# A fused linear-attention and routed-FFN block: output products in fp32r terms with streamed weights, and a third head's mask on ScalarE

## The reference

```python
# attention: 16 heads of 16, feature width 64
q, k, v = heads(x @ Wq + bq), heads(x @ Wk + bk), heads(x @ Wv + bv)
qp, kp = relu(q @ rw) + EPS, relu(k @ rw) + EPS          # per head
kv = kp.T @ v                                            # summed over the whole sequence
out = (qp @ kv) / (qp @ kp.sum() + EPS)
x = layernorm(x + out @ Wo + bo)
# FFN: gated MLP of width 1024, plus experts
sim = (x @ Wq) . keys                # 2 halves x 4 heads x 64 keys
sx, sy = top_8 of each half;  scores = top_8 of the 64 sums sx + sy      # per head
w = silu(x @ down_embed[idx]) * softmax(scores)          # 4 heads x 8 experts of 1024
y = (silu(x @ Wg + bg) * (x @ Wu + bu)) @ Wd + bd  +  sum of w * up_embed[idx]
x = layernorm(x + y)
```

## Time and profile before

| | us |
|---|---|
| median of 3 runs | 3515.26 (3514.70 to 3517.06) |
| the profiled execution | 3515.04, its span 3513.3 |
| PE busy | 3414.6 (97%) |
| DVE busy | 2830.2 (81%) |
| ACT busy | 1990.0 (57%) |
| POOL busy | 1163.0 (33%) |
| output products, lines 744 and 746 | 622.3 and 609.1 of PE's busy time |
| chain that ended last | PE 81%, DVE 8%, ACT 6%, POOL 2% |

### The profile page before, as it was taken

One profiled execution on the slowest core, in us unless ns is written; L12 is line 12 of the kernel. 1 busy time (PEld: TensorE's weight loads), 2 busy tenths in 40 slices (PEclk: granted clock), 3 DMA queues, 4 the chain that ended last, 5 costly groups with the idle time before them and its releaser, 6 DMA issues.

```text
span 3513.3 us, 49408 instructions
## 1 busy us (share of the span) xinstructions
PE 3414.6 (97%) x18400; PEld 2693.9 (77%) x18400; DVE 2830.2 (81%) x5316; ACT 1990.0 (57%) x2886; POOL 1163.0 (33%) x724
## 2 busy tenths in 40 slices
PE   8779999999999999999999999999999999999988
PEld 6457877777877777877777877777777778777777
DVE  4688888888888888888888887888878888888873
ACT  4456556555566555556555655555655564555551
POOL 0233333333333333333333333333333333343330
PEclk9899999999999999999999999999999999999999
DMA  4000000000000000000000000000000000000000
GB/s 121 18 13 19 7 13 19 19 19 19 7 13 19 19 19 14 12 13 19 19 19 9 17 13 19 19 19 7 19 13 19 19 13 7 13 13 7 12 7 12
DMA packets 23452, 60.84 MB, mean 17 GB/s; under 512 B 5808, under 2 KB 10160, under 8 KB 23216
## 3 DMA queue, kind: packets, MB, share of 16 engines
q1 hardware_dynamic: 23216, 57.69, 5.0%
HBM read 40.91 MB, written 16.78 MB: 16 GB/s over the span
## 4 chain that ended last, share of the span: by engine, by line
PE 81%; DVE 8%; ACT 6%; issue 3%; POOL 2%; DMA 0%; SPq 0%; POOLq 0%; DVEq 0%; ACTq 0%
PE ring L651 25%; PE y_bank L744 11%; PE y_bank L746 10%; PE step_bank L553 6%; PE step_bank L545 5%; PE step_bank L651 4%; PE step_bank L589 3%; PE step_bank L581 3%; PE step_bank L680 3%; DVE prob L1144 3%; PE step_bank L670 3%; PE step_bank L724 3%; PE step_bank L539 2%; POOL grid L464 2%; PE y_bank L740 1%
## 5 line engine op out<-in xcount | busy, mean ns | idle before, releaser
L464 POOL TENSOR_TENSOR grid<-ex 128x1024 f32<-128x1024 f32 x512 | 997.6, 1956 | 1507.5 <-ACT ex L877 730.6
L744 PE MATMUL y_bank<-wd_sb,gate 128*128 128x256 f32 x2048 | 622.3, 386 | 1.7 <-DVE wexp L1166 1.7
L746 PE MATMUL y_bank<-up_sb,wexp 128*128 128x256 f32 x2048 | 609.1, 379 | 0.0
L1144 DVE SCALAR_TENSOR_TENSOR prob<-grid,narrow,prob 128x1024 f32<-128x1024 f32 x256 | 552.2, 2157 | 9.0
L651 PE MATMUL ring<-x1T_hl,downT_hl 128*128 128x512 f32 x1536 | 420.8, 409 | 16.8 <-ACT gate L901 16.7
L651 PE MATMUL ring<-x1T_hl,wg_hl 128*128 128x512 f32 x1536 | 431.2, 416 | 3.8 <-DVE gate L1160 3.8
L1131 DVE SCALAR_TENSOR_TENSOR grid<-grid,best 128x1024 f32<-128x1024 f32 x256 | 327.2, 1278 | 131.8 <-POOL grid L464 128.8
L746 PEld LDWEIGHTS y_bank<-up_sb,wexp 128*128 128x128 f32 x2048 | 389.2, 190 | 53.0
L651 PE MATMUL ring<-x1T_hl,wu_hl 128*128 128x512 f32 x1536 | 421.4, 409 | 0.0
L744 PEld LDWEIGHTS y_bank<-wd_sb,gate 128*128 128x128 f32 x2048 | 354.0, 190 | 53.3 <-issue 25.2
L651 PEld LDWEIGHTS ring<-x1T_hl,wu_hl 128*128 128x128 f32 x1536 | 282.0, 188 | 119.8 <-issue 42.9
(11 more groups left out here) (169 smaller groups left out, 5578.7 us busy)
## 6 DMA issues: line engine op xcount, KB each, us to landing
xb<-in_L_attn_x SPq DMA_DIRECT2D x34, 512.0 KB, 3.5
out_y<-x SPq DMA_DIRECT2D x32, 512.0 KB, 2.9
xa<-in_L_attn_x SPq DMA_DIRECT2D x30, 512.0 KB, 4.2
prob<-in_L_ffn_down_embed SPq DMA_DIRECT2D x1, 1024.0 KB, 6.0
prob<-in_L_ffn_Wg SPq DMA_DIRECT2D x1, 1024.0 KB, 8.8
prob<-in_L_ffn_Wu SPq DMA_DIRECT2D x1, 1024.0 KB, 10.9
wd_sb<-in_L_ffn_Wd SPq DMA_DIRECT2D x1, 1024.0 KB, 11.3
up_sb<-in_L_ffn_up_embed SPq DMA_DIRECT2D x1, 1024.0 KB, 11.8
```

Source lines behind the costliest of these rows:

```text
L464: pool.tensor_tensor(grid[:, h % 2], bcast(ex[:, h, 0:NX].unsqueeze(2), [P, NX, NK]), bcast(ex[:, RH + h, 0:NK].unsqueeze(1), [P, NX, NK]) ...
L744: pe.matmul(rows, gate[:, c % 2, t * P:(t + 1) * P], wd_sb[:, c, :], start=(c == 0 and t % 2 == 0), stop=False, skip_group_check=True)
L746: mm = pe.matmul(rows, wexp[:, c % 2, t * P:(t + 1) * P], up_sb[:, c, :], start=False, stop=(c == C - 1), skip_group_check=True)
L1144: ins = dve.scalar_tensor_tensor(out=row, in0=g, scalar=rz[:, h:h + 1], in1=row, op0=ALU.mult, op1=ALU.add, accum_out=mass[:, 0:1] if h == ...
```

## The change

Both output products are made of three fp32r terms. Per chunk there are 12 gate terms (four tiles: high x high, high x low, low x high) and behind them 12 terms of the expert weight, instead of four tiles with one fp32 product of each kind. The splits of `gate` and `wexp` are made in each slot: `gate_top(c)` and `wexp_top(c-1)` are casts by ACT, `ff_low` is DVE's difference. The gate's low part stands behind `ff_wexp(c)` on DVE; the expert weight's stands at the head of the next slot, ahead of `ff_h`, but for chunk 7, where it is made in slot 7 itself, with its cast ahead of the mask of head 1. `gate` and `wexp` themselves lie in free parts of `prob`, and the masks get waits for them.

Wd and up_embed split take twice the room. They are split in the prologue (eight rounds of cast, low part and store, PREP_STEPS = 18), kept in a DRAM tensor, and streamed back, one chunk of 512 KB at a time into a ring of two slots, by transfers that POOL issues (`ff_stream`), each at the head of a slot and behind the wait that chunk c-2 has been used.

ACT masks head 2 too, right behind head 1. DVE's keep of head 2 goes; its add becomes a plain add and moves from behind add 1 to behind keep 3.

```diff
@@ -46,7 +46,7 @@
-    ACT_HEADS, STEEP = 2, float(2 ** 30)
+    ACT_HEADS, STEEP = 3, float(2 ** 30)
@@ -87,7 +87,8 @@
-        wd_sb, up_sb = sb("wd_sb", P, C, D), sb("up_sb", P, C, D)
+        wdup = sb("wdup", P, 2, 4, D, dt=F32R)
+        wdup_kept = nc.dram_tensor("wdup_kept", [C, P, 4, D], F32).ap()
@@ -119,20 +120,31 @@
-        gate = sb("gate", P, 2, G)
-        wexp = sb("wexp", P, 2, G)
+        gate_hi, gate_lo = sb("gate_hi", P, 2, G, dt=F32R), sb("gate_lo", P, 2, G, dt=F32R)
+        wexp_hi, wexp_lo = sb("wexp_hi", P, 2, G, dt=F32R), sb("wexp_lo", P, 2, G, dt=F32R)
...
@@ -345,9 +364,11 @@
-        PREP_STEPS, PREP_WG, PREP_WU = 11, 9, 10
+        PREP_STEPS, PREP_WG, PREP_WU = 18, 9, 10
+        PREP_WD = {11: (0,), 12: (1,), 13: (2,), 14: (3,)}
+        PREP_UP = {14: (0,), 15: (1,), 16: (2,), 17: (3,)}
...
-        W_ALL = 16 * (4 + 4 + 2 + 4 + 2)
+        W_ALL = 16 * (4 + 2 + 2 + 4 + 2)
@@ -380,6 +401,14 @@
+            sp.wait_ge(prep_full, 4)
+            sp.dma_start(wd_rows, Wd.rearrange("(c p) n -> p c n", p=P)).then_inc(wd_staged, 16)
+            sp.wait_ge(low_ready, 2)
+            sp.dma_start(up_rows, up.rearrange("(c p) n -> p c n", p=P)).then_inc(up_staged, 16)
+            for w, i in [(0, 0), (0, 1), (0, 2), (0, 3), (1, 0), (1, 1), (1, 2), (1, 3)]:
+                sp.wait_ge((wd_low, up_low)[w], i + 1)
+                sp.dma_start(wdup_kept[2 * i:2 * i + 2, :, 2 * w:2 * w + 2, :].rearrange("c p w d -> p c w d"),
+                             wdup[:, :, 2 * w:2 * w + 2, :].bitcast(F32)).then_inc((wd_kept, up_kept)[w], 16)
@@ -470,9 +499,20 @@
+                def ff_stream(c):
+                    g = n * C + c
+                    if g == 0:
+                        pool.wait_ge(wd_kept, 16 * (C // 2))
+                        pool.wait_ge(up_kept, 16 * (C // 2))
+                    wait(pool, y_full, g - 1)
+                    pool.dma_start(wdup[:, c % 2], wdup_kept[c]).then_inc(wdup_loaded[c % 2], 16)
...
+                    if ff:
+                        ff_stream(c)
@@ -725,15 +765,19 @@
-                def ff_out(c, pair):
-                    if pair == 0:
+                def ff_out(c, half):
+                    first, last = c == half == 0, c == C - 1 and half == 1
+                    if half == 0:
...
-                        pe.wait_ge(h_ready, n * C + c + 1)
-                        pe.wait_ge(*drained("pt", n, c))
-                    for t in (2 * pair, 2 * pair + 1):
-                        rows = y_bank[pair][:, (t % 2) * D:(t % 2 + 1) * D]
-                        if c == C - 2:
+                        pe.wait_ge(wdup_loaded[c % 2], 16 * ((n * C + c) // 2 + 1))
+                        pe.wait_ge(gate_split, n * C + c + 1)
+                    else:
+                        pe.wait_ge(wexp_split, n * C + c + 1)
+                    hi, lo = ((gate_hi, gate_lo), (wexp_hi, wexp_lo))[half]
+                    for t in range(T):
+                        rows = y_bank[t // 2][:, (t % 2) * D:(t % 2 + 1) * D]
+                        if c == C - 2 and half == 0:
@@ -741,11 +785,11 @@
-                        pe.matmul(rows, gate[:, c % 2, t * P:(t + 1) * P], wd_sb[:, c, :],
-                                  start=(c == 0 and t % 2 == 0), stop=False, skip_group_check=True)
-                        mm = pe.matmul(rows, wexp[:, c % 2, t * P:(t + 1) * P], up_sb[:, c, :],
-                                       start=False, stop=(c == C - 1), skip_group_check=True)
-                    if pair == 1:
+                        for i, (src, w) in enumerate([(hi, 0), (hi, 1), (lo, 0)]):
+                            mm = pe.matmul(rows, src[:, c % 2, t * P:(t + 1) * P], wdup[:, c % 2, 2 * half + w, :],
+                                           start=(first and t % 2 == 0 and i == 0), stop=(last and i == 2),
+                                           skip_group_check=True)
+                    if half == 1:
@@ -799,6 +843,16 @@
+                for i in PREP_WD.get(k, ()):
+                    act.wait_ge(wd_staged, 16)
+                    wait(act, wd_kept, 16 * i)
+                    act.copy(wdup[:, :, 0, :], wd_rows[:, 2 * i:2 * i + 2, :]).then_inc(wd_high, 1)
+                for i in PREP_UP.get(k, ()):
+                    act.wait_ge(up_staged, 16)
+                    wait(act, up_kept, 16 * i)
+                    act.copy(wdup[:, :, 2, :], up_rows[:, 2 * i:2 * i + 2, :]).then_inc(up_high, 1)
+                if k > PREP_WU:
+                    return
@@ -887,10 +941,13 @@
-                    g = grid[:, h].rearrange("p a b -> p (a b)")
+                    g = grid[:, h % 2].rearrange("p a b -> p (a b)")
...
+                        act.wait_ge(wexp_split, (s - 1) * C)
+                    if t == 2 and h == 0 and ff:
+                        act.wait_ge(wexp_split, n * C + C // 2)
@@ -898,12 +955,22 @@
-                    act.activation(gate[:, c % 2], ring[c % 2][:], ACT.Silu,
+                    if c == 0:
+                        wait(act, wexp_split, n * C)
+                    act.activation(gate(par, c), ring[c % 2][:], ACT.Silu,
...
-                    act.activation(wexp[:, c % 2], ring[c % 2][:], ACT.Silu).then_inc(ring_act, 1)
+                    act.activation(wexp(par, c), ring[c % 2][:], ACT.Silu).then_inc(ring_act, 1)
+                def gate_top(c):
+                    act.wait_ge(h_ready, n * C + c + 1)
+                    act.copy(gate_hi[:, c % 2], gate(par, c)).then_inc(gate_high, 1)
+                def wexp_top(c):
+                    act.wait_ge(*drained("pt", n, c))
+                    act.copy(wexp_hi[:, c % 2], wexp(par, c)).then_inc(wexp_high, 1)
@@ -911,6 +978,8 @@
                         ff_gate(c)
+                        if c:
+                            wexp_top(c - 1)
                     if at:
@@ -921,11 +990,14 @@
                         ff_dots(c)
+                        gate_top(c)
                     if at:
...
                             at_use(*use)
+                    if ff and c == C - 1:
+                        wexp_top(c)
                     if rt and c % 2:
-                        mask(c // 2, 1)
+                        mask(c // 2, 1), mask(c // 2, 2)
                     if rt and c % 2 == 0 and c:
...
@@ -1137,7 +1215,9 @@
-                        dve.wait_ge(masked, s * (ACT_HEADS * T) + t * ACT_HEADS + ACT_HEADS)
+                        dve.wait_ge(masked, s * (ACT_HEADS * T) + t * ACT_HEADS + h + 1)
+                        if h > 1:
+                            rt_steps.wait(marks["add", h - 1])
@@ -1157,14 +1237,18 @@
-                    dve.scalar_tensor_tensor(out=gate[:, c % 2], in0=ring[1 - c % 2][:], scalar=bu_sb[:, c:c + 1],
-                                             in1=gate[:, c % 2], op0=ALU.add, op1=ALU.mult).then_inc(h_ready, 1)
+                    dve.scalar_tensor_tensor(out=gate(par, c), in0=ring[1 - c % 2][:], scalar=bu_sb[:, c:c + 1],
+                                             in1=gate(par, c), op0=ALU.add, op1=ALU.mult).then_inc(h_ready, 1)
...
-                    read_by(dve.tensor_tensor(wexp[:, c % 2], bank_of("pt", n, c)[:], wexp[:, c % 2], ALU.mult),
+                    read_by(dve.tensor_tensor(wexp(par, c), bank_of("pt", n, c)[:], wexp(par, c), ALU.mult),
...
+                def ff_low(whole, high_part, low_part, s_high, s_split, c):
+                    dve.wait_ge(s_high, n * C + c + 1)
+                    low(low_part[:, c % 2], whole(par, c), high_part[:, c % 2], s_split)
@@ -1199,6 +1283,8 @@
                         blocks(it // BG - 1)
+                    if ff and c:
+                        ff_low(wexp, wexp_hi, wexp_lo, wexp_high, wexp_split, c - 1)
                     uses(AT_EARLY[c])
@@ -1208,16 +1294,20 @@
                     uses(AT_MID[c])
-                    if rt and odd:
-                        keep(t, 2)
+                    if ff and c == C - 1:
+                        ff_wexp(c)
                     if at and c == 6:
...
                         constants(it // BG - 1)
+                    if ff and c < C - 1:
+                        ff_wexp(c)
                     if ff:
-                        ff_wexp(c)
+                        ff_low(gate, gate_hi, gate_lo, gate_high, gate_split, c)
+                        if c == C - 1:
+                            ff_low(wexp, wexp_hi, wexp_lo, wexp_high, wexp_split, c)
                     if rt and odd:
-                        add_head(t, 1), add_head(t, 2)
+                        add_head(t, 1)
                     uses(KV_LATE[c])
@@ -1232,7 +1322,7 @@
                     if rt and odd:
-                        add_head(t, 3), clamp(t)
+                        add_head(t, 2), add_head(t, 3), clamp(t)
                 assert not rt or rt_steps.k == RT_STEPS
```

31 lines of the change are left out of this document (25 added, 6 removed).

## The result

The changed kernel takes 3661.72 us (median of 4 runs, 3658.22 to 3662.69) against 3515.45 of the kernel before on the same chip: ratio 1.0414, interval [1.0396, 1.0432], slower by 146 us. The profiled execution has a span of 3656.4, 143.1 more than before.

A forecast was written before the change was run, and what follows sets the result against it. PE was taken to bound a full iteration (104.6 us), the routing chain behind it at 98.3. PE falls to 99.1, the chain rises to 107.85; with other iterations and prologue +20, together +122: 3637 us, range 3480 to 3720.

The forecast's parts named there:

- The forecast case: Whole kernel: routing chain at 107.85 us passes PE's 99.1 in a full iteration; 3637 us, case range 3570 to 3720, chance 0.60.
- The bound before: Full iteration before: PE busy for all 104.6 us, routing chain hidden behind it at 98.3, between 92.9 and 104.6.
- Part 1: Output products on PE: new terms 0.115 us each, 2.77 a chunk for 3.46; PE falls from 104.6 to 99.1 an iteration.
- The rival with weight loads as the pace: PE's output terms: each pays its 0.19 us load, PE 113.4 an iteration, 3780 us in all; chance 0.03.
- Part 4: Slot 0: the gate's cast delays ACT's copy, q and the exp; 5.35 us from gate product against 3.9, +1.45.
- Part 2: ACT ahead of the second mask: casts and a third lift add 1.3, 1.3, 1.45 and 3.15 us, together 7.2.
- Part 3: DVE from the second mask to the next gate product: +0.4, +0.5, +0.5 and -0.5 us, together +0.9.
- a rival: PE's new pauses bring its clock down, or the weight stream is late: 3715 us and more; chance 0.08.
- Part 5: Prologue: eight rounds of cast, low part and store, about 4.3 us per wait; +20 us, between 0 and 25.
- Part 6: Weight stream: 256 transfers of 512 KB issued by POOL, costed at nothing.
- The rest: Other iterations: fold 0; without key/value work three by 9.5 and one with fold +8; routing and FFN alone +8; last -5.5.
- rival (b): Balance: slot 0's and ACT's added delays cost half, chain 103.2 us; about 3510 us, 3480 to 3560; chance 0.17.

The follow-up runs named there:

- e12: e9 with the masks of before (two heads by ACT, keep of head 2 by DVE), the edit of e2; 3389.13 us, 0.9636 of the kernel before.
- e1: Changed kernel with slot 0's cast of the gate's high part on ACT behind the copies of the transposed blocks; 3578.56 us, 1.0176 of before.
- e2: Changed kernel with the masks as before: two heads by ACT, keep of head 2 by DVE; 3797.32 us, 1.0794 of before.
- e3: Changed kernel without the third term (activation's low part times weight's high part) of each product, casts and low parts still made; 3663.57 us, 1.0416 of before.
- e9: Changed kernel without any split of the two activations: two terms per product, no casts or low parts in the loop, three masked heads kept; 3313.60 us, 0.9418 of before.
- e5: Changed kernel with the first iteration's two loads of x issued by SP ahead of the eight stores of split weights; 3650.85 us, 1.0380 of before.
- e6: Changed kernel with gate casts of slots 1, 3, 5 behind head 1's mask, their low parts behind add 1 and the sum of kv; 3651.79 us, 1.0383 of before.
- e13: e9 with the first loads of x ahead of the stores and up_embed's prologue rounds and stores between those of Wd; 3299.06 us, 0.9378 of before.
- e7: Changed kernel with both casts of slot 7 behind head 1's mask on ACT and both low parts behind add 1 on DVE; 3591.38 us, 1.0205 of before.
- e8: Changed kernel with the four edits of e1, e5, e6 and e7 together; 3573.99 us, 1.0158 of before.

## Why the prediction was right, and where it was not

The forecast case came: the routing chain took over from PE, 3637 was forecast and 3661.72 measured, +122 and +146.

*The bound before.* The chain of a full iteration, hidden under PE's 104.6, was estimated at 98.3; e12 shows 99.3 (key/value work adds 6.2 to it, not 5.4). Here the sign of the result was decided: 5.3 us of slack, and 9.2 us put on it.

*Part 1.* 1.45 and 1.36 for the two halves, 2.81 a chunk for the 2.77 forecast. The rival with weight loads as the pace is out: the load of a term lasts 188 ns, a term 0.12. The Trainium skill, "TensorE: Matmul & The Clock Gate", Part 3 "The mechanism", lists loads as overlapping matmuls in flight only across row groups, though it also has them pulled ahead into a background weight buffer; for terms that use all rows this trace disagrees with the first and does not speak against the second.

*Parts 2 to 4, pair by pair*, after less e12 beside the forecast: pair 1 +4.3 (3.15), pair 2 +1.4 (1.8), pair 3 +0.5 (1.95), pair 4 +3.0 (2.65); together +9.2 for 9.55. The sum is right by errors of opposite sign, which is luck. Part by part (each a stretch of the chain, us):

| | pair 1 | 2 | 3 | 4 | sum |
|---|---|---|---|---|---|
| gate product to exp (part 4), forecast | 1.45 | 0 | 0 | 0 | 1.45 |
| measured | 4.0 | 0 | 0 | 0 | 4.0 |
| exp to the second mask's end (part 2), forecast | 1.3 | 1.3 | 1.45 | 3.15 | 7.2 |
| measured | 0 | 1.2 | 1.2 | 4.3 | 6.75 |
| mask's end to the next gate product (part 3), forecast | 0.4 | 0.5 | 0.5 | -0.5 | 0.9 |
| measured | 0.3 | 0.2 | -0.7 | -1.3 | -1.5 |

- *Part 2* held in pairs 2 and 3. In pair 1 the added work on ACT vanished ahead of the mask, in pair 4 the wait for DVE and the two casts cost 1.1 more than forecast.
- *Part 4 was mis-sized.* The link through slot 0 has the shape that was forecast, and in the two iterations in which q keeps the upper clock its length too: 5.40 us from gate product to exp, for 5.35. On the mean it is 6.7, because q mostly runs at half the clock (3.38 for 1.96 in the rows above), which I had only in a rival. The link before was mis-read as well: I took 3.9 from an iteration that PE held up, and bare it is 2.71 (e12). In e1 the link is gone and pair 1 is 3.3 shorter.
- *Part 3 had the wrong sign, and with it the masks.* I priced the third head as a lift more on ACT and +0.4 behind the mask. The 2x2 of the table says -2.4 without splits and -4.7 with them. The step that failed is the one that followed ACT's queue alone to the second mask: DVE's keep of head 2 stood ahead of add 1 as well, so that in e12 add 1 came 1.85 us behind the mask in pair 3 and 0.54 in pair 4 (with splits, e2, 1.16 in pair 2 and 2.37 in pair 3). With the keep gone it comes 0.98 and 0.03 behind it in pairs 3 and 4. In pair 4 with splits the keep also stood ahead of the product that ACT casts ahead of its mask, and the mask ends 1.25 later in e2 than in the changed kernel. What the missing keep saves is more than the new wait for POOL's spread costs. In pair 1 the masks of before are shorter with splits (29.70 for 30.56) only because q runs faster there, 2.30 us on the mean for 3.27.
- The splits were accordingly dearer than forecast: 12.2 (e3 less e9), not some 9.

*Part 5, mis-sized*: the first copy +28.2 for +20. The rounds are 4.18 for 4.3 (a store is 512 KB, like the row that priced it, not the 256 that I wrote); left out were x's loads, which SP issues behind the stores. With these ahead (e5) it is +20.3.

*Part 6 held*: 256 transfers by POOL land in 3.6 us, and POOL spends 0.59 us on the issue:

```profile
2139.09 0.59 POOL L509 DMA_DIRECT2D wdup<-wdup_kept  x1
```

Where the profile names what PE's terms waited for, it is DVE's low parts, 26 us in the whole span, and never a transfer (32 us of short gaps have no name there). The Trainium skill, "SBUF — State Buffer", "DVE blocks DMA" note, warns that POOL can't write descriptors while DVE runs an operation in a 2-port mode; the runs here show no late transfer with DVE busy for 78% of the span, but not whether any of its operations is in such a mode.

*The rest*: iterations without key/value work +14.1, +13.9 and +12.0 for 9.5 (the fourth pair is 31.96 or 30 there for 26.73); with the fold -1.4 for 0; iteration 32 +8.3 for 8; 36 +4.8 for 8; 37 -5.2 for -5.5. In rival (b), half of parts 2 and 4 makes a chain of 103.5, not 103.2.

Of the experiments' theories, A (all loss in slot 0) falls with e1, e3 and e9, and B as I stated it (every ACT instruction ahead of the mask counts in full) with e2 and e6: the chain passes ACT and DVE in turn, and both run close to it. Open is why the clock fell in 17 of the 19 iterations and not in the other two, whose pauses are as long.

## What to carry to other kernels

When the busiest engine is relieved, the price of the helpers (casts, low parts, masks) is read from the chain that runs close behind it, with every engine that it passes, and an iteration in which the busy engine has less to do shows that chain bare. A cast put into an in-order queue costs what stands behind it, and on TensorE a pause can cost twice, as in slot 0 here: once as a pause and once as the clock afterwards. If three fp32r terms are too dear for their split, two terms with only the weight split (e13, with the prologue in another order too: 3299 us, 6.2% below the kernel before, the activation rounded to fp32r) keep the cheap matmuls and need no split in the loop.

## What the runs showed of the hardware

- After an idle time of 3.68 us PE was granted 0.50 of its clock (the 1.2 GHz level) and had the upper level back from 2104.6 on; q took 3.38 us instead of 1.96. So it went in 17 of 19 full iterations with pauses of 3.55 to 3.98 us; in two, with 3.61 and 3.63, q took 1.95, and so it did in all 19 of e7, with 1.5 on the mean.
- POOL's spread (128x1024) takes 1.91 us beside the sum of kv (one operand in PSUM) and 2.88 in slot 3 of e6 and e8, with a DVE low part of two SBUF operands beside it that takes its usual 0.68. Elsewhere the low part pays: in slot 3 of the changed kernel two spreads keep 3.99, and the low part that starts beside the second takes 1.60:

```profile
2135.15 3.99 POOL L493 TENSOR_TENSOR grid<-ex 128x1024 f32<-128x1024 f32 x2 [10.28 <-ACT ex L931]
```

```profile
2138.09 1.60 DVE L1026 TENSOR_TENSOR wexp_lo<-prob,wexp_hi 128x512 fp32r<-128x512 f32 x1 [1.17 <-ACT wexp_hi L973]
```

- The Trainium skill, "SBUF — State Buffer", "SBUF: two separate sides", calls the port that the two share an exclusive lock, held by whichever starts first. The traces agree that one holds the other up; the order they bear out in the rows above, not in e8, where by the profile's starts the spread came first (2105.31 for 2105.75) and was still the one to get longer.
- A cast of 128x512 from SBUF to fp32r takes 0.62 us on ACT, 0.52 to 0.60 from start to start.
